# First batch normalised by halves, its conv on VectorE, and the normalised x added to the output projection by TensorE

## The chip, the cores and the metric

The kernel runs on one core of one Trainium2 chip. The metric is the device time of one execution in microseconds, median over several runs. The core's engines work side by side and hand over through semaphores: TensorE (PE in the profile; PEld is its weight load) multiplies and transposes into PSUM, VectorE (DVE) and ScalarE (ACT) work element by element, GpSimd (POOL) does small arithmetic, constants and the accumulating DMAs, SyncE (SP) issues all other DMAs.

## The reference

Two blocks with residuals over x of shape [4, 1024, 128]: a "ripple" attention and a mixture of experts, each between two layernorms. Cut to what matters here:

```python
def _ripple(x, Wqkv, Wo, conv_w):                 # C = 128, 8 heads of 16
    q, k, v = jnp.split(x @ Wqkv, 3, axis=-1)     # qh, kh, vh: the same by heads
    # each position attends to itself and to those 1, 2, 4, ..., 512 before it
    tele = einsum(softmax(q . k[pos - off]), v[pos - off])
    conv = depthwise_conv(v, conv_w)              # 7 taps, causal
    fq, fk = elu(qh) + 1, elu(kh) + 1
    low = fq @ (fk^T v) / (fq . sum(fk) + 1e-6)   # linear attention
    return (tele + conv + low) @ Wo

def _L0_attn_ref(x, ...):
    return x + _ripple(x, Wqkv, Wo, conv_w)

h = _layernorm(x)                                 # "the normalised x"
x = x + _layernorm(_L0_attn_ref(h, ...))
x = x + _layernorm(_L0_ffn_ref(_layernorm(x), ...))
```

So the normalised x enters twice: into the projections, and as the residual that is added to the output projection before the second layernorm.

## The kernel before

Everything is fp32 (the gates are spread in bf16 parts). A batch has 1,024 tokens, eight tiles (NT) of 128; a unit u is half a batch, four tiles (TPH): units 2b and 2b+1 belong to batch b. The loop over b runs five times; its pass b does the attention of batch b beside the experts (ffn) of units 2b-2 and 2b-1. Every engine has one program, written out by hand in the order in which it shall run, and waits where its operands come from another engine. Nothing is reordered: what stands behind a waiting instruction waits too.

Attention of a batch, with the names that matter:

- `stats` (VectorE, bn and mv), `ln1` (GpSimd: rstd by pow, nmr), `normalise1` (ScalarE): the normalised x, tile by tile, in `xn`. TensorE turns it (`turn_x`) into the two banks of `psA`, ScalarE copies it to `xnT`, channels on partitions. `project_k`, `project_q`, `project_v` multiply by wqkv, in the two halves of psA; ScalarE copies the results to kT, qT and vT. While batch b is at work, this head part of batch b+1 is done in between. For batch 0 it stands ahead of all.
- `features`: exp and relu of k and q on ScalarE, minimum and sum on VectorE (fkT, fqT). `token_major_v` and `token_major_fk`: turned back by TensorE and copied by ScalarE into v_tok and fk_tok. `linear_state` (TensorE, in psY) and kv (VectorE).
- `shift_v` (SyncE): 18 DMAs copy v_tok, shifted by 1 to 64 rows, into `v_shift`, 3.5 MB or so. VectorE needs them for the first `weigh`.
- `products` (VectorE, q times shifted k, three groups), `sum_heads` (TensorE), `scores` (ScalarE), `turn_scores` (TensorE), `softmax_logits` (VectorE, begins with zden), `exponentials` (ScalarE), `softmax_weights` (VectorE, begins with den), `weigh_low` and eight `weigh` (VectorE), eight `sum_terms` (TensorE, up to twelve transposes into psH, accumulated).
- The conv: `scale_taps` (ScalarE) scales vT by each of the seven taps into seven buffers (`tap_home`: convT, tapT[0], tapT[1], xnT, kexp, qexp, tapT[0] again). GpSimd adds them with six DMAs of 512 KB that accumulate in SBUF (`sum_taps_first`, `_second`, `_third`). They all run while v_shift is being filled. `features(b+1)` waits until kexp has been added.
- `add_conv(b, half)` (VectorE): hT = psH + convT. `output(b, half)` (TensorE): hT times Wo, into psY for both halves, so the second waits until the first was read. `add_normed(b, half)` (VectorE): yc = psY + xn_res, where xn_res is a copy of xn that ScalarE makes (`keep_normed`, 128x1024). `norm2(u)` (ScalarE): sums of the squares of yc. `ln2` (GpSimd), `residual(u)` (VectorE): x2 = yc * rstd2 + x_res. The residual of unit 2b stands behind the last weigh of batch b, that of unit 2b+1 in the next pass behind `products(b+1, 1)`.

After x2 come norm3, the gates, the hidden layer in psF, `experts_out` and norm4. The last units use psH and psY for gates and hidden layers too. `keep_busy` issues idle transposes of ident, into psH before the third sum of heads.

## Time and profile before

| | us |
|---|---|
| three runs | 316.63, 318.48, 319.97 |
| median | 318.48 |
| profiled execution | 320.01 |
| its span | 318.0 |

| engine | busy us | share of the span |
|---|---|---|
| PE | 256.4 | 81% |
| PEld | 173.4 | 55% |
| DVE | 234.7 | 74% |
| ACT | 205.7 | 65% |
| POOL | 90.1 | 28% |

The page's strip of 40 slices (7.95 us each), a digit is tenths busy:

```profile
PE   6664977089579779997897799989798899888894
DVE  5049936298996669889988699399976897936842
ACT  1578655047737974699869963798488615375851
PEclk9785797789959989999999969999799589799998
DMA  7300999900789940121989830106889601000003
```

DMA stands for the sixteen DMA engines together. Batch 0 is in the slices up to about the tenth; the DMA engines are full in slices 5 to 8 and VectorE's digit falls to 2 in the eighth. PEclk is the granted clock of TensorE: 10 tenths (shown as 9) are 2.4 GHz, 5 tenths 1.2 GHz.

Durations in a timeline are those of single instructions or of merged rows; neighbouring ones on an engine overlap by a tenth of a microsecond or so, so the distance from start to start is a little less than the duration. A matmul of fp32 that isn't a transpose has two records, a transpose one.

### The profile page before, as it was taken

How to read it: one execution, taken by the hardware profiler on the slowest of the kernel's cores; microseconds unless marked ns; L12 is line 12 of the kernel's file. 1: busy time of each engine (PE TensorE's matmuls, PEld its weight loads, DVE VectorE, ACT ScalarE, POOL GpSimd, SP SyncE). 2: the span in 40 equal slices, each digit the busy share in tenths (PEclk: the TensorE clock that was granted, in tenths of full speed). 3: DMA queues.
4: the chain of work that ended last, by engine and by line, in shares of the span. 5: the costliest groups of instructions: out<-in, count | busy, mean ns of one | idle time of the engine just before them, and what ended most of it. 6: DMA issues, size and time to landing. Idle time of an engine off the chain costs nothing.

```text
span 318.0 us, 4568 instructions
## 1 busy us (share of the span) xinstructions
PE 256.4 (81%) x1527; PEld 173.4 (55%) x1527; DVE 234.7 (74%) x567; ACT 205.7 (65%) x471; POOL 90.1 (28%) x153
## 2 busy tenths in 40 slices
PE   6664977089579779997897799989798899888894
PEld 6323443087345437766553448658445296774283
DVE  5049936298996669889988699399976897936842
ACT  1578655047737974699869963798488615375851
POOL 3912150101514310304566002125741103131013
PEclk9785797789959989999999969999799589799998
DMA  7300999900789940121989830106889601000003
GB/s 215 94 0 16 220 225 227 226 7 0 159 235 240 200 82 3 33 67 25 224 240 205 195 68 0 34 2 136 241 231 227 117 2 33 0 3 0 1 2 99
DMA packets 23809, 34.46 MB, mean 108 GB/s; under 512 B 3989, under 2 KB 17134, under 8 KB 23786
## 3 DMA queue, kind: packets, MB, share of 16 engines
q1 hardware_dynamic: 20330, 21.59, 24.2%
q0 software_dynamic: 3456, 12.58, 21.5%
q8 instruction: 12, 0.20, 0.3%
q14 instruction: 11, 0.09, 0.1%
HBM read 5.07 MB, written 2.10 MB: 23 GB/s over the span
## 4 chain that ended last, share of the span: by engine, by line
PE 43%; ACT 29%; SPq 8%; DVE 7%; POOL 6%; issue 3%; DMA 3%; POOLq 0%; DVEq 0%; ACTq 0%
PE psH L1215 9%; PE psA L1135 6%; PE psY L1312 5%; PE psF L1276 5%; ACT xn L633 4%; SPq L341 3%; POOL rstd L427 3%; SPq L344 3%; ACT xn L539 3%; ACT squares L626 2%; PE psY L1164 2%; PE psA L1127 2%; PE psY L1226 2%; PE psF L1255 2%; DMA v_shift<-v_tok 2%
## 5 line engine op out<-in xcount | busy, mean ns | idle before, releaser
L264 DVE TENSOR_TENSOR prods<-qT,kT 128x1024 f32<-128x1024 f32 (+1 forms) x44 | 48.8, 1166 | 13.6 <-ACT qT L527 13.6
L425 POOL TENSOR_SCALAR var<-ss 128x4 f32<-128x4 f32 (+1 forms) x25 | 11.1, 443 | 123.1 <-ACT squares L679 62.1
L1215 PE MATMUL psH<-ident,prods 128*128 128x128 f32 x324 | 43.1, 285 | 0.0
L1215 PEld LDWEIGHTS psH<-ident,prods 128*128 128x128 f32 x324 | 39.3, 149 | 2.3 <-issue 2.3
L427 POOL TENSOR_TENSOR rstd<-var,neg_half 128x4 f32<-128x4 f32 (+2 forms) x29 | 37.2, 1283 | 2.4
L902 DVE TENSOR_TENSOR prods<-v_shift,prob 128x896 f32<-128x896 f32 x32 | 35.8, 1119 | 0.0
L1276 PE MATMUL psF<-x3T,w 128*128 128x512 f32 x58 | 31.7, 661 | 0.1
L1016 DVE TENSOR_TENSOR hid<-hid,psG 128x512 f32<-128x512 f32 x32 | 20.8, 684 | 14.9 <-PE psG L1298 14.3
L1135 PE MATMUL psA<-xnT,wqkv 128*128 128x512 f32 x48 | 30.0, 771 | 2.1 <-ACT xnT L527 2.1
L1183 PE MATMUL psA<-prods,slot_sel 128*32 128x512 f32 x168 | 25.3, 656 | 4.4 <-DVE prods L264 3.0
L439 POOL DMA_DIRECT2D convT<-tapT x12 | 10.9, 907 | 60.8 <-DMA convT<-tapT 29.4
L902 DVE TENSOR_TENSOR prods<-v_tok,prob 128x128 f32<-128x128 f32 (+2 forms) x60 | 20.8, 373 | 7.5 <-DMA v_shift<-v_tok 7.5
L655 ACT ACTIVATE hid<-psF,b1c 128x512 f32<-128x512 f32 x29 | 18.8, 686 | 2.6 <-PE psF L1276 2.4
L1312 PEld LDWEIGHTS psY<-w,hid 128*128 128x128 f32 x140 | 17.7, 207 | 3.6 <-DVE prods L886 2.7
L1212 PE MATMUL psH<-ident,prods 128*128 128x128 f32 x32 | 9.7, 302 | 12.1 <-DVE prods L902 9.6
L539 ACT ACTIVATE xn<-x_in,nmr,rstd 128x128 f32<-128x128 f32 x32 | 13.0, 484 | 9.2 <-POOL nmr L436 9.2
L1312 PE MATMUL psY<-w,hid 128*128 128x128 f32 x140 | 18.0, 292 | 1.1 <-DVE prods L886 1.1
L1276 PEld LDWEIGHTS psF<-x3T,w 128*128 128x128 f32 x58 | 10.9, 210 | 14.2 <-issue 11.6
L1135 PEld LDWEIGHTS psA<-xnT,wqkv 128*128 128x128 f32 x48 | 10.6, 243 | 14.6 <-issue 6.5
L620 ACT ACTIVATE squares<-yc 128x128 f32<-128x128 f32 x32 | 9.4, 298 | 8.9 <-DVE yc L925 8.9
L1212 PEld LDWEIGHTS psH<-ident,prods 128*128 128x128 f32 x32 | 4.7, 147 | 17.6 <-DVE prods L902 13.1
L581 ACT ACTIVATE tapT<-vT,cw 128x1024 f32<-128x1024 f32 x12 | 13.2, 1135 | 0.1
(199 smaller groups left out, 557.1 us busy)
## 6 DMA issues: line engine op xcount, KB each, us to landing
v_shift<-v_tok SPq DMA_DIRECT2D x20, 448.0 KB
convT<-tapT POOLq DMA_DIRECT2D x12, 512.0 KB, 4.6
x_in<-L_attn_x SPq DMA_DIRECT2D x4, 512.0 KB, 3.6
x_res<-L_attn_x SPq DMA_DIRECT2D x4, 512.0 KB, 9.2
tapT<-xnT POOLq DMA_DIRECT2D x4, 512.0 KB, 9.9
convT<-kexp POOLq DMA_DIRECT2D x4, 512.0 KB, 7.5
tapT<-qexp POOLq DMA_DIRECT2D x4, 512.0 KB, 9.7
out<-y_out SPq DMA_DIRECT2D x7, 256.0 KB, 2.3
```

What stands on the lines that cost most here:

```text
L264: return eng.tensor_tensor(prods[:, QUADS * (s % 2) + q, t0:T], qT[:, t0:T], kT[:, PRE - off + t0:PRE - off + T], ALU.mult)
L427: return nc.gpsimd.tensor_tensor(rstd[:, cols], var[:, cols], neg_half[:, cols], ALU.pow)
L539: nc.scalar.activation(xn[:, j, :], x_in[:, j, :], ACT.Identity, bias=nmr1[:, j:j + 1], scale=rstd1[:, j:j + 1]).then_inc(xn_ready, 1)
L655: nc.scalar.activation(hid[:, c, half_cols(u)], hidden_bank(u, c), ACT.Gelu, bias=b1c[:, c:c + 1]).then_inc(hidden_free, 1)
L902: return nc.vector.tensor_tensor(dst, src.rearrange("p m (h d) -> p m h d", d=HD), w, ALU.mult)
L1016: nc.vector.tensor_tensor(hid[:, c, cols], hid[:, c, cols], psG[:, c % 2, :], ALU.mult).then_inc(gated, 1)
L1135: pe.matmul(psA[:, half, :], wqkv[:, bass.ts(part, P)], xnT[:, bass.ts(half, HALF)], start=True, stop=True).then_inc(psA_full, 1)
L1183: ins = pe.matmul(psA[32 * q:32 * q + 32, half, :], ksum_sel[:] if low else slot_sel[:, s, :], fqT[:, cols] if low else prods[:, QUADS * ( ...
L1212: pe.matmul(dst, low_terms[:, j, :], ident[:], is_transpose=True, start=True, stop=False)
L1215: ins = pe.matmul(dst, terms[:, j % TERM_BUFS, m, :], ident[:], is_transpose=True, start=False, stop=(m == live[-1]))
L1276: pe.matmul(hidden_bank(u, c), w1[:, bass.ts(c, P)], x3T[:, half_cols(u)], start=True, stop=True).then_inc(hidden_full, 1)
L1312: ins = pe.matmul(output_tile(u, n), hid[:, c, bass.ts(j, P)], w2[:, c, :], start=(c == CH - 1), stop=(c == CH - 2))
```

## The change

Three things are changed together.

1. **Batch 0's layernorm by halves.** `first_norm` (VectorE) takes statistics and variance of four tiles, then of the other four; GpSimd only does the pow (`first_rstds`), VectorE makes nmr. ScalarE normalises the first four tiles when their nmr is there. VectorE instead of ScalarE copies xnT out of PSUM.
2. **Batch 0's conv on VectorE.** `first_conv` is one multiplication by a scalar per partition and six fused multiply-adds into convT[0], each waiting for the one before: four ahead of `softmax_logits(0)`, three between it and `softmax_weights(0)`. Batch 0 has no scaled taps and no accumulating DMAs. The other batches keep theirs, with a buffer tapT[2] in place of xnT.
3. **The normalised x is added by TensorE.** xnT exists twice (by the batch's parity) and lives until the output projection. `output` issues for each tile the matmul by Wo and then a transpose of the tile of xnT that accumulates onto it. The second half goes to psH in place of psY. yc, xn_res, `add_normed` and `keep_normed` are gone; norm2 and residual read psY and psH. `keep_busy` before the third sum of heads writes to psG. Unit 6's front (turned x, gate logits, logits) uses psF, and its first hidden chunk waits until the logits have been read.

The diff's core:

```diff
             def sum_taps_first(b):
-                pool.wait_ge(tap_scaled, upto(b, TAPS, 4))
+                pool.wait_ge(tap_scaled, upto(b - 1, TAPS, 4))
...
-            ln1(0)
+            first_rstds()
             constants()
             more_constants()
-            sum_taps_first(0)
...
-            def keep_normed(b):
-
-                act.wait_ge(yc_ready, upto(b, 2, 0))
-                copy(xn_res[:], xn[:]).then_inc(xn_kept, 1)
...
             def norm2(u):
-                act.wait_ge(yc_ready, u + 1)
-                for j in unit_tiles(u):
-                    last = nc.scalar.activation(squares[:, j, :], yc[:, j, :], ACT.Square, accum_out=ss2[:, j:j + 1])
+                act.wait_ge(y_ready, u + 1)
+                for n, j in enumerate(unit_tiles(u)):
+                    last = nc.scalar.activation(squares[:, j, :], attended(u % 2)[:, bass.ts(n, P)], ACT.Square,
+                                                accum_out=ss2[:, j:j + 1])
...
+            def first_norm():
+
+                dve.wait_ge(x_in_ld, N_DMA)
+                first_chain.start(dve, 0)
+                for half in range(2):
+                    tiles = range(half * TPH, (half + 1) * TPH)
+                    cols = slice(half * TPH, (half + 1) * TPH)
+                    for j in tiles:
+                        last = nc.vector.bn_stats(bn[:, j, :], x_in[:, j, :])
+                    first_chain(last)
+                    for j in tiles:
+                        last = nc.vector.bn_aggr(mv[:, j, :], bn[:, j, :])
+                    first_chain(last)
+                    nc.vector.tensor_scalar(var1[:, cols], mv[:, cols, 1], EPS, None, ALU.add).then_inc(first_var, 1)
+                for half in range(2):
+                    cols = slice(half * TPH, (half + 1) * TPH)
+                    dve.wait_ge(first_rstd, half + 1)
+                    nc.vector.scalar_tensor_tensor(out=nmr1[:, cols], in0=mv[:, cols, 0], scalar=-1.0,
+                                                   in1=rstd1[:, cols], op0=ALU.mult,
+                                                   op1=ALU.mult).then_inc(first_normed, 1)
+                nc.vector.tensor_scalar(neg_mean[:, 0, :], mv[:, :, 0], -1.0, None, ALU.mult)
+                for half in range(2):
+                    dve.wait_ge(psA_full, filled(-1, PSA_X, half))
+                    nc.vector.tensor_copy(xnT[0][:, bass.ts(half, HALF)], psA[:, half, :]).then_inc(psA_free, 1)
...
+            def first_conv(shifts):
+
+                if 0 in shifts:
+                    dve.wait_ge(psA_free, freed(-1, PSA_V, 1))
+                    dve.wait_ge(conv_ld, N_DMA)
+                    conv_chain.start(dve, 0)
+                for shift in shifts:
+                    v, w = vT[:, VPRE - shift:VPRE - shift + T], cw[:, TAPS - 1 - shift:TAPS - shift]
+                    if shift == 0:
+                        conv_chain(nc.vector.tensor_scalar(convT[0][:], v, w, None, ALU.mult))
+                    else:
+                        conv_chain(nc.vector.scalar_tensor_tensor(out=convT[0][:], in0=v, scalar=w, in1=convT[0][:],
+                                                                  op0=ALU.mult, op1=ALU.add))
...
-            def add_normed(b, half):
...
+                    if b == 0:
+                        first_conv(range(0, 4))
                     softmax_logits(b)
+                    if b == 0:
+                        first_conv(range(4, TAPS))
...
             def linear_state(b, first):
                 if not first:
-                    pe.wait_ge(yc_ready, upto(b, 2, 0))
+                    pe.wait_ge(x2_ready, upto(b, NT, -TPH))
...
             def output(b, half):
                 pe.wait_ge(hT_ready, upto(b, 2, half + 1))
-                if half:
-                    pe.wait_ge(yc_ready, upto(b, 2, 1))
-                elif b:
+                if b and not half:
                     pe.wait_ge(out_scaled, b)
                 for j in range(TPH * half, TPH * (half + 1)):
-                    ins = pe.matmul(psY[:, bass.ts(j % TPH, P)], hT[:, bass.ts(j, P)], wo[:], start=True, stop=True)
+                    dst = attended(half)[:, bass.ts(j % TPH, P)]
+                    pe.matmul(dst, hT[:, bass.ts(j, P)], wo[:], start=True, stop=False)
+                    ins = pe.matmul(dst, xnT[b % 2][:, bass.ts(j, P)], ident[:], is_transpose=True, start=False, stop=True)
                 ins.then_inc(y_ready, 1)
...
+                    elif k >= 0:
+                        pe.wait_ge(front_free, upto(u, N_FRONT, N_FRONT - k))
```

How the instructions stand on the engines, at three places. VectorE in batch 0, before, from the last group of products (L264; ksum_sel and kv belong to the linear state) to the softmax's weights:

```order
L264 TENSOR_TENSOR prods<-qT,kT 128x1024 x6
L847 TENSOR_SCALAR ksum_sel<-head_sel,ksum 128x8
L850 TENSOR_TENSOR kv<-psY,head_mask 128x128
L858 TENSOR_SCALAR zden<-psA 128x64
L860 TENSOR_TENSOR prob<-psA,mask 128x384 x2
L867 TENSOR_REDUCE top<-prob 128x64
L868 TENSOR_TENSOR prob<-prob,top 128x768
L873 TENSOR_REDUCE den<-prob 128x64
L874 RECIPROCAL rden<-den 128x64
```

And after the change (the lines of the file are other ones):

```order
L269 TENSOR_TENSOR prods<-qT,kT 128x1024 x6
L885 TENSOR_SCALAR ksum_sel<-head_sel,ksum 128x8
L888 TENSOR_TENSOR kv<-psY,head_mask 128x128
L962 TENSOR_SCALAR convT<-vT,cw 128x1024
L964 SCALAR_TENSOR_TENSOR convT<-vT,cw,convT 128x1024 x3
L896 TENSOR_SCALAR zden<-psA 128x64
L898 TENSOR_TENSOR prob<-psA,mask 128x384 x2
L905 TENSOR_REDUCE top<-prob 128x64
L906 TENSOR_TENSOR prob<-prob,top 128x768
L964 SCALAR_TENSOR_TENSOR convT<-vT,cw,convT 128x1024 x3
L911 TENSOR_REDUCE den<-prob 128x64
```

Four conv instructions stand between kv and zden, three between the last step of the logits (prob<-prob,top) and den.

ScalarE in batch 0, before, from the copy of vT to the copy of the scores (prods is where scoresT lies):

```order
L527 ACTIVATE vT<-psA 128x512 x2
L581 ACTIVATE convT<-vT,cw 128x1024
L581 ACTIVATE tapT<-vT,cw 128x1024 x2
L581 ACTIVATE xnT<-vT,cw 128x1024
L527 ACTIVATE v_tok<-psA 128x512 x2
L527 ACTIVATE fk_tok<-psA 128x512 x2
L527 ACTIVATE xn_res<-xn 128x1024
L581 ACTIVATE kexp<-vT,cw 128x1024
L581 ACTIVATE qexp<-vT,cw 128x1024
L581 ACTIVATE tapT<-vT,cw 128x1024
L527 ACTIVATE prods<-psA 128x512 x2
```

And after:

```order
L541 ACTIVATE vT<-psA 128x512 x2
L541 ACTIVATE v_tok<-psA 128x512 x2
L541 ACTIVATE fk_tok<-psA 128x512 x2
L541 ACTIVATE prods<-psA 128x512 x2
L555 ACTIVATE xn<-x_in,nmr,rstd 128x128 x8
```

The seven scalings and the copy to xn_res are gone; v_tok follows vT at once.

TensorE at the end of batch 0, before, from the first half of the output projection (psY<-wo,prods; prods is where hT lies) to the turns of the next batch's v:

```order
L1226 MATMUL psY<-wo,prods 128x128 x4
L1135 MATMUL psA<-xnT,wqkv 128x512 x2
L1212 MATMUL psH<-ident,prods 128x128
L1215 MATMUL psH<-ident,prods 128x128 x11
L1212 MATMUL psH<-ident,prods 128x128
L1215 MATMUL psH<-ident,prods 128x128 x11
L1212 MATMUL psH<-ident,prods 128x128
L1215 MATMUL psH<-ident,prods 128x128 x11
L1226 MATMUL psY<-wo,prods 128x128 x4
L1127 MATMUL psA<-ident,vT 128x128 x8
```

And after:

```order
L1273 MATMUL psY<-wo,prods 128x128
L1274 MATMUL psY<-ident,xnT 128x128
L1183 MATMUL psA<-xnT,wqkv 128x512 x2
L1260 MATMUL psH<-ident,prods 128x128
L1263 MATMUL psH<-ident,prods 128x128 x11
L1260 MATMUL psH<-ident,prods 128x128
L1263 MATMUL psH<-ident,prods 128x128 x11
L1260 MATMUL psH<-ident,prods 128x128
L1263 MATMUL psH<-ident,prods 128x128 x11
L1273 MATMUL psH<-wo,prods 128x128
L1274 MATMUL psH<-ident,xnT 128x128
L1273 MATMUL psH<-wo,prods 128x128
```

Shown of after are the last pairs of the first half and the first of the second half; a half is four pairs of a matmul by wo and a transpose of xnT, and the second half goes to psH. The projection of the next batch's v and three sums of terms stand between the halves, as before.

## Rows read from the trace of the kernel before

**Rows 1.** The chain that ended last: start us, us, what

```profile
56.03 5.58 DMA v_shift<-v_tok
...
93.28 3.41 PE psY L1164 x16
...
97.36 0.94 ACT xn_res L527
...
160.30 1.78 PE psY L1164 x16
...
162.66 0.94 ACT xn_res L527
...
280.22 0.70 DVE yc L925
```

**Rows 2.** Timeline of VectorE in batch 0: start, us, instruction, idle before, releaser

```profile
25.97 1.23 DVE L832 SCALAR_TENSOR_TENSOR fqT<-qexp,fqT 128x1024 f32<-128x1024 f32 x1
...
39.18 0.28 DVE L850 TENSOR_TENSOR kv<-psY,head_mask 128x128 f32<-128x128 f32 x1
...
44.54 0.23 DVE L858 TENSOR_SCALAR zden<-psA 128x64 f32<-128x64 f32 x1 [5.07 <-PE psA L1127]
...
49.15 1.53 DVE L873 TENSOR_REDUCE den<-prob 128x64 f32<-128x768 f32 x1 [0.91 <-ACT prob L608]
...
61.64 0.29 DVE L902 TENSOR_TENSOR prods<-v_tok,prob 128x128 f32<-128x128 f32 x1 [7.47 <-DMA v_shift<-v_tok]
```

**Rows 3.** DMA queues, 30 to 62 us: packets, MB, share of 16 engines

```profile
q0 software_dynamic: 791, 2.91, 49.4%
...
q1 hardware_dynamic: 1994, 4.03, 46.7%
```

**Rows 4.** Timeline of SyncE's queue, first and last of 18 issues in batch 0

```profile
30.33 0.58 SPq L341 DMA_DIRECT2D v_shift<-v_tok  x1
...
56.03 0.60 SPq L344 DMA_DIRECT2D v_shift<-v_tok  x1
```

**Rows 5.** Timeline of the head, all engines

```profile
4.38 1.64 DVE L801 BATCH_NORM_STATS2 bn<-x_in 128x6 f32<-128x128 f32 x8 [0.82 <-DMA x_in<-L_attn_x]
...
6.05 0.64 DVE L805 BATCH_NORM_AGGREGATE mv<-bn 128x2 f32<-128x6 f32 x8
...
7.33 1.66 POOL L427 TENSOR_TENSOR rstd<-var,neg_half 128x8 f32<-128x8 f32 x1
...
9.31 3.19 ACT L539 ACTIVATE xn<-x_in,nmr,rstd 128x128 f32<-128x128 f32 x8 [7.24 <-POOL nmr L436]
...
11.10 0.66 PE L1127 MATMUL psA<-ident,xn 128*128 128x128 f32 x4 [2.30 <-ACT xn L539]
...
13.46 7.87 PE L1135 MATMUL psA<-xnT,wqkv 128*128 128x512 f32 x12
...
19.55 0.60 ACT L527 ACTIVATE qT<-psA 128x512 f32<-128x512 f32 x1 [0.26 <-PE psA L1135]
```

**Rows 6.** Table by stretches: busy us (instructions) per engine, PEclk, DMA share, GB/s

```profile
9.00:11.00 2.00, 0.00 (x0) 0.00 (x0) 0.00 (x0) 1.69 (x5) 1.79 (x9) 1.00 0.20 17
...
13.00:18.20 5.20, 5.20 (x10) 2.37 (x9) 0.00 (x0) 1.79 (x3) 4.33 (x24) 0.50 0.34 101
...
66.00:68.00 2.00, 2.00 (x20) 2.00 (x19) 2.00 (x5) 2.00 (x3) 0.00 (x0) 0.96 0.01 4
```

**Rows 7.** Timeline of TensorE: end of batch 0, and two projections in batch 1

```profile
71.43 1.06 PE L1226 MATMUL psY<-wo,prods 128*128 128x128 f32 x8
...
76.78 1.36 PE L1215 MATMUL psH<-ident,prods 128*128 128x128 f32 x11
...
128.14 1.88 PE L1135 MATMUL psA<-xnT,wqkv 128*128 128x512 f32 x4
```

**Rows 8.** Groups by line and form: busy us, mean ns of one, idle before

```profile
L581 ACT ACTIVATE tapT<-vT,cw 128x1024 f32<-128x1024 f32 x12 | 13.2, 1135 | 0.1
...
L1026 DVE SCALAR_TENSOR_TENSOR y_out<-psG,rstd,x 128x128 f32<-128x128 f32 x8 | 2.2, 341 | 1.2 <-POOL rstd L427 1.2
```

119 lines of the change are left out of this document (63 added, 56 removed).

## The prediction

> **What bounds the kernel now.** I read these views in this order: the chain that ended last, the timeline of each engine over batch 0, the DMA queues over the same stretch, and the table by stretches. The chain [rows 1] changes engine all the time: no engine is the bound of the whole program, so an edit is worth what it takes off this chain and nothing else. Four places of it concern the change: a DMA wait in batch 0 that ends at 61.61 us, the copy of xn into xn_res on ScalarE in batches 1 and 2 (only these two of the four copies are listed), and the addition yc on VectorE in the last batch.
>
> VectorE in batch 0 [rows 2]: from the first products to kv at 39.46 us it is busy; then it waits 5.07 us for the turned scores, 0.91 us for the exponentials and 7.47 us for the shifted copies of v. The reason for the last wait is in [rows 3]: between 30 and 62 us the software queue (the six accumulating transfers of the conv) holds 49.4% of the sixteen engines and the hardware queue (v_shift, and one x_in) 46.7%. SyncE issues the 18 transfers of v_shift from 30.33 to 56.63 us [rows 4].
>
> In the head, VectorE, GpSimd and ScalarE work one after the other before TensorE gets its first tile at 11.10 us; the projections start at 13.46 us and their last copy on ScalarE ends at 20.15 us [rows 5]. TensorE's granted clock is 1.00 in 9 to 11 us and 0.50 (1.2 GHz) from 13 to 18.2 us [rows 6].
>
> **The change part by part.** Durations are those of the profiled execution (320.0 us; span 318.0).
>
> *Head by halves.* Before: bn 1.64, mv 0.64, GpSimd's pow on eight columns 1.66, around them small ones, and xn starts at 9.31 [rows 5]. After, the first half needs 0.82 + 0.32 + about 0.2 on VectorE (var) and about 1.2 on GpSimd for four columns (between half of 1.66 and 1.66; I take 1.2), then nmr, 0.2 and hand-overs of 0.2: xn can start at 4.4 + 1.1 + 0.2 + 1.2 + 0.4 = 7.3 to 7.5. The second pow starts at about 7.2 and is there before ScalarE ends its fourth tile, so all eight tiles are 1.9 earlier. VectorE takes xnT out of PSUM in place of ScalarE, on an idle engine: nothing. Second half and projections follow: 13.46 becomes 11.35. **-2.1 us.** SyncE's queue: load_next(0) moves with xn, nothing waits for it.
>
> *TensorE's clock in the projections.* After the warm-up TensorE now waits until 11.10 us and the clock then falls. With the change it waits from 8.8 to about 9.1, works 0.7, waits 0.9 and goes on. I take it that the clock stays at 2.4 GHz. Two projections of 512 columns take 1.88 us at full clock [rows 7], four 3.6, plus the last copy 0.6: 4.2 in place of 20.15 - 13.46 = 6.7. **-2.5 us**; nothing if the clock falls all the same.
>
> The Trainium skill says in "TensorE: Matmul & The Clock Gate", Part 4, that transposes do not count as TensorE being busy for the gate, and by that the warm-up and the earlier turns could not hold the clock. This trace does not agree: in 66 to 68 us TensorE did nothing but transposes and the clock rose to a mean of 0.96 [rows 6].
>
> *ScalarE in batch 0* loses seven scalings of 1.14 us [rows 8] and one copy. Four of them, 4.2 us as they overlap, stood ahead of v_tok; TensorE's turn of v needs some 0.7 of that, so v_tok, fk_tok and SyncE's first v_shift are another 3.5 earlier. VectorE does not wait for those: it is busy up to 39.46 in any case, only moved by the head.
>
> *VectorE's conv and the transfers.* Seven instructions on 1,024 elements. Their nearest row is the fused one with two tensors, 1.23 us [rows 2]; each waits for the one before, so 1.25 from start to start, the first (one tensor) between 0.6 and 1.15. First group: 1.15 + 3 x 1.25 = 4.9, in the wait of 5.07: hidden. If TensorE should deliver the scores sooner, VectorE comes first there, no loss. Second group: 3 x 1.25 = 3.75, of which the wait of 0.91 hides one part: +2.85. What it buys: the six accumulating transfers go. v_shift starts 3.5 + 4.6 earlier, at 22, and even at the old pace (26.3 to issue, 5 to land) is there at 53 us; at its own share (0.467 x 32 = 15 us) at 39. It is needed at 61.64 - 7.47 + 2.85 - 4.6 = 52.4. So the wait of 7.47 goes, at worst but 1 us. Together 2.85 - 7.47 = **-4.6 us**. GpSimd's queue loses six issues; its ln1(1) comes earlier, which nobody waits for.
>
> *The output projection.* 32 transposes more. In the sum of a tile eleven follow each other in 1.36 us with the tail of the last, so 0.11 each [rows 7]: four are +0.44 per half. The upper bound is a matmul's own 0.27 (eight records, four matmuls, in 1.06 [rows 7]); I take the lower, since the kind is the same. Where do they lie on the path? End of batch 0: TensorE goes without a gap from the first output (71.43) over the projection of v and three sums to 78.14, and VectorE's conv addition waits for that: +0.44. The add of yc that is removed there does not help, TensorE is last. The second output of batches 0, 1 and 2 stands ahead of the turn of v, which leads to the next batch's ScalarE chain: +0.44 three times. The first output of batches 1 and 2 delays the gate spread by 0.44, and VectorE loses yc (0.7) behind it: nothing. Last batch: second output +0.44. Sum **+2.2 us**. Squares and residual now read PSUM. The nearest row is the fused instruction at the end of the kernel, with the same operands but one in PSUM: 341 ns for 128 columns [rows 8]. Should a read from PSUM cost a tenth more, that is 0.1 us for four: nothing. The bank psY is free again when residual has run, some 15 us before linear_state wants it; psH likewise.
>
> *The copies xn_res.* Two pieces of 0.94 lie on the chain [rows 1], in stretches where ScalarE goes almost without a gap up to the exponentials: **-1.9 us**. In batch 3 TensorE is last: nothing. *The last yc*: 0.73 from its start to the squares of ScalarE [rows 1]: **-0.7 us**. In the tail, hidden(6, 0) now waits for gexp, 0.4 later, and ends just before the turn of the last half: nothing, 0.3 if late.
>
> Sum: -2.1 - 2.5 - 4.6 + 2.2 - 1.9 - 0.7 = **-9.6 us**: 310.4 from the profiled execution, 308.9 from the median of 318.5. The profiled one is the slowest of four, so a part of what it shows to be gained may be its own bad luck; I forecast between the two, 309.5.
>
> **The rivals.**
> 1. *The clock falls in the projections all the same.* For it: TensorE works only 0.7 of about 1.8 us there. Against: the wait of 2.3 is gone. Time 309.5 + 2.5 = 312.
> 2. *The clock falls elsewhere.* The linear state of batch 1 took 3.41 us at half clock, that of batch 2 1.78 at full clock [rows 1], with the same instructions: 1.6 for the lower clock, and I estimate as much again for its neighbours (gate logits, turns), 3.3 in all. A chain moved by some us can put one more such stretch into batches 2 or 3: 309.5 + 3.3 to + 5.8 = 313 to 315. The other way, batch 1 loses its slow stretch: 309.5 - 3.3 = 306.
> 3. *The change doesn't do what it says*: v_shift stays as late behind VectorE as it was, because SyncE's issue and not the accumulating queue paces it. Then the wait ends at 61.64 - 4.6 - 3.5 = 53.5, since the scaling no longer holds up v_tok, and the loss is 1.1 us: 310.6. To lose the whole term the landing would have to move not at all: 309.5 + 8 = 317.5.
> 4. *Slower.* A transpose behind an fp32 matmul into the same bank may not pipeline. Five halves are on the path with four pairs each; the gain is eaten when one pair costs (9.0 + 2.2) / 20 = 0.56 us more than the matmul alone. At the matmul's own 0.27 [rows 7] it would be 309.5 + 20 x 0.16 = 312.7, and slower by over 1% needs 0.72. Nothing in the rows comes near; 323 as its time.
>
> **How the numbers follow.** Forecast 0.50 at 309.5; clock falling in the head 0.22 at 312; one more slow stretch 0.13 at 313 to 315; batch 1 at full clock 0.07 at 306; change without its main effect 0.05 at 317.5; slower 0.03 at 323. The range from 305 to 315 leaves out the last two and some edges. A measurement can tell about 1% from no change, here 315.3 and 321.7. Faster: the first four, less some edge, 0.87; same 0.09; slower 0.04, the fourth rival with a little for what I have not seen.
>
> **What would show it.** VectorE: no wait for v_shift at its first weighing, that one at about 52 us; the conv's instructions near 1.2 us, four of them ahead of zden with no or a small wait. Head: first xn near 7.4, projections from 11.4, their clock 1.00; last q copy near 15.5. TensorE: eight matmul records and four transposes of an output half within 1.6 us. No wait of ScalarE's squares for yc. Wrong would be: fused instructions well over 1.3 us; a clock of 0.5 in the projections; linear_state or low waiting for x2; a half of the output over 2 us.

## The result and the profile after

The changed kernel takes 304.35 us (median of four, 302.13 to 305.5) where the kernel before, run beside it, took 318.24 (316.63 to 319.97): 0.9554 of its time, 95% interval 0.948 to 0.963, a gain of 13.9 us. The forecast was 309.5 with a range down to 305: right in sign, wrong in size. The profiled execution took 304.41 us. Medians below are of all executions of a kernel; ratios, and the gains given with them, leave out those that were over 1.5% slower than its fastest, and are taken to the kernel before run beside it.

The page of the changed kernel: span, busy time, granted clock in tenths over 40 slices, shares of the chain.

```profile
span 302.7 us, 4600 instructions
...
PE 248.6 (82%) x1559; PEld 170.7 (56%) x1559; DVE 240.0 (79%) x573; ACT 192.6 (64%) x458; POOL 84.4 (28%) x145
...
PEclk9989599599979979999999989999999799999999
...
PE 42%; ACT 26%; DVE 21%; POOL 5%; issue 4%; DMA 1%; POOLq 0%; DVEq 0%; ACTq 0%
```

The head in its timeline, all engines; it answers to [rows 5]:

```profile
7.40 3.19 ACT L555 ACTIVATE xn<-x_in,nmr,rstd 128x128 f32<-128x128 f32 x8 [5.33 <-DVE nmr L826]
...
9.19 0.63 PE L1175 MATMUL psA<-ident,xn 128*128 128x128 f32 x4 [1.32 <-ACT xn L555]
...
11.13 5.70 PE L1183 MATMUL psA<-xnT,wqkv 128*128 128x512 f32 x12
...
15.05 0.60 ACT L541 ACTIVATE qT<-psA 128x512 f32<-128x512 f32 x1 [0.36 <-PE psA L1183]
```

xn starts at 7.40 (forecast 7.3 to 7.5), the projections at 11.13 (11.35), the last copy of q ends at 15.65 (15.5). The first products start at 15.79 in place of 20.28, 4.5 us earlier; 4.6 were forecast.

VectorE in batch 0; it answers to [rows 2]:

```profile
35.36 0.74 DVE L962 TENSOR_SCALAR convT<-vT,cw 128x1024 f32<-128x1024 f32 x1
36.13 3.93 DVE L964 SCALAR_TENSOR_TENSOR convT<-vT,cw,convT 128x1024 f32<-128x1024 f32 x3
40.96 0.23 DVE L896 TENSOR_SCALAR zden<-psA 128x64 f32<-128x64 f32 x1 [0.90 <-PE psA L1175]
...
44.60 3.92 DVE L964 SCALAR_TENSOR_TENSOR convT<-vT,cw,convT 128x1024 f32<-128x1024 f32 x3
48.55 1.53 DVE L911 TENSOR_REDUCE den<-prob 128x64 f32<-128x768 f32 x1
...
53.49 0.28 DVE L940 TENSOR_TENSOR prods<-v_tok,prob 128x128 f32<-128x128 f32 x1
```

The wait of 7.47 us for v_shift is gone, the first weighing stands at 53.49 (before 61.64, forecast 52), and the conv's fused instructions take 1.32 us from start to start (forecast 1.25). That the wait goes was forecast rightly; the first weighing came 1.5 us later than forecast.

Where the rest came from is seen when the span is cut at events that both timelines have: VectorE's two additions of the conv (add_conv) in each batch, ScalarE's gexp, VectorE's den. The last column is the prediction's sum, put into the same cuts.

| stretch | before | after | difference | forecast |
|---|---|---|---|---|
| start to second add_conv of batch 0 | 78.18 | 71.84 | -6.34 | -8.8 |
| three boundaries: second add_conv to gexp | 53.20 | 48.45 | **-4.75** | **+1.3** |
| gexp to den, batches 1 to 3 | 56.52 | 54.79 | -1.73 | -1.9 |
| den to first add_conv, batches 1 to 3 | 56.39 | 55.33 | -1.06 | 0 |
| first to second add_conv, batches 1 to 3 | 33.99 | 32.69 | **-1.30** | **0** |
| last add_conv to the end | 39.72 | 39.60 | -0.12 | -0.3 |
| span | 318.0 | 302.7 | -15.3 | -9.6 |

The error sits at the boundaries between batches and, smaller, between the two additions; in batch 0 the changed kernel gained 2.5 us less than forecast. TensorE's part of the transposes has the forecast size. The second half of the output projection of batch 0 in its timeline, before, and after (the first pair and the last, then the turn of v):

```profile
78.93 1.16 PE L1226 MATMUL psY<-wo,prods 128*128 128x128 f32 x8 [0.79 <-DVE prods L919]
79.93 1.04 PE L1127 MATMUL psA<-ident,vT 128*128 128x128 f32 x8
```

```profile
72.58 0.49 PE L1273 MATMUL psH<-wo,prods 128*128 128x128 f32 x2 [0.78 <-DVE prods L972]
72.91 0.27 PE L1274 MATMUL psH<-ident,xnT 128*128 128x128 f32 x1
...
73.91 0.27 PE L1274 MATMUL psH<-ident,xnT 128*128 128x128 f32 x1
74.02 1.04 PE L1175 MATMUL psA<-ident,vT 128*128 128x128 f32 x8
```

From the first matmul to the turn of v it is 1.44 us, and 1.00 in the kernel before: +0.44. So something else took some 6 us off the stretches in bold, less 1.48 that the third boundary of this one execution had too much (below).

### The profile page after: what moved, and what is told of

Read it like the earlier page. It is cut to its first block, busy times and chain, and to the rows that moved or that the text cites. A ratio compares the mean times of both kernels' runs of the same rounds, so it can differ in the third digit from the quotient of the medians.

```text
span 302.7 us, 4600 instructions
## 1 busy us (share of the span) xinstructions
PE 248.6 (82%) x1559; PEld 170.7 (56%) x1559; DVE 240.0 (79%) x573; ACT 192.6 (64%) x458; POOL 84.4 (28%) x145
## 4 chain that ended last, share of the span: by engine, by line
PE 42%; ACT 26%; DVE 21%; POOL 5%; issue 4%; DMA 1%; POOLq 0%; DVEq 0%; ACTq 0%
PE psH L1263 7%; PE psA L1183 5%; PE psF L1322 5%; PE psY L1358 4%; DVE prods L940 4%; ACT xn L645 3%; PE psA L1231 3%; ACT xn L555 3%; DVE prods L269 3%; PE psA L1358 3%; ACT squares L638 3%; POOL rstd L435 2%; PE psY L1212 2%; PE psA L1175 2%; POOL var L433 2%
## 5 line engine op out<-in xcount | busy, mean ns | idle before, releaser
L1263 PEld LDWEIGHTS psH<-ident,prods 128*128 128x128 f32 x324 | 39.1, 148 | 2.3 <-issue 2.3
L435 POOL TENSOR_TENSOR rstd<-var,neg_half 128x4 f32<-128x4 f32 (+2 forms) x28 | 32.3, 1155 | 2.3
L1183 PE MATMUL psA<-xnT,wqkv 128*128 128x512 f32 x48 | 26.2, 683 | 3.3 <-ACT xnT L541 3.3
L454 POOL DMA_DIRECT2D convT<-tapT x9 | 8.2, 913 | 43.3 <-DMA convT<-tapT 26.0
L1358 PEld LDWEIGHTS psY<-w,hid 128*128 128x128 f32 x140 | 16.1, 192 | 3.6 <-DVE prods L924 2.6
L1358 PE MATMUL psY<-w,hid 128*128 128x128 f32 x140 | 16.4, 276 | 1.2 <-DVE prods L924 1.2
L1183 PEld LDWEIGHTS psA<-xnT,wqkv 128*128 128x128 f32 x48 | 8.5, 203 | 13.7 <-ACT xnT L541 4.8
L1231 PEld LDWEIGHTS psA<-prods,slot_sel 128*32 128x32 f32 x168 | 5.2, 112 | 16.4 <-issue 8.5
L1367 PEld LDWEIGHTS psG<-ident 128*128 128x128 f32 x76 | 10.8, 168 | 6.3 <-issue 3.2
L1367 PE MATMUL psG<-ident 128*128 128x128 f32 x76 | 11.5, 317 | 3.1 <-POOL ident L389 3.1
```

Of the source, the lines that this page charges most:

```text
L435: return nc.gpsimd.tensor_tensor(rstd[:, cols], var[:, cols], neg_half[:, cols], ALU.pow)
L1183: pe.matmul(psA[:, half, :], wqkv[:, bass.ts(part, P)], xnT[(b + 1) % 2][:, bass.ts(half, HALF)], start=True, stop=True).then_inc(psA_full, 1)
L1231: ins = pe.matmul(psA[32 * q:32 * q + 32, half, :], ksum_sel[:] if low else slot_sel[:, s, :], fqT[:, cols] if low else prods[:, QUADS * ( ...
L1263: ins = pe.matmul(dst, terms[:, j % TERM_BUFS, m, :], ident[:], is_transpose=True, start=False, stop=(m == live[-1]))
L1358: ins = pe.matmul(output_tile(u, n), hid[:, c, bass.ts(j, P)], w2[:, c, :], start=(c == CH - 1), stop=(c == CH - 2))
L1367: pe.transpose(bank[:, bass.ts(k % TPH, P)], ident[:], ident[:])
```

## Experiments

### Each part alone

Each is one of the three pieces of the diff put into the kernel before, here in short:

```diff
+first_norm(), first_rstds()                 # head_only: in place of stats(0), ln1(0)
+first_conv(range(0, 4)), first_conv(range(4, TAPS))   # conv_only: in place of scale_taps(0), sum_taps(0)
+pe.matmul(dst, xnT[b % 2][...], ident[:], is_transpose=True, start=False, stop=True)   # add_only: no keep_normed, no add_normed
```

> Part 1 alone on the kernel before: batch 0's layernorm by halves, everything else as before. By the prediction's own steps: first products on VectorE at about 15.7 us in place of 20.28 and 4.6 us less in all (2.1 for the halves, 2.5 for the clock in the projections), since the wait for v_shift moves with it. Rival (the clock falls in the projections all the same): only 2.1 less, and a granted clock of 0.50 at 13 us.

314.64 us, ratio 0.987 (0.981 to 0.992): -4.3 us.

> Part 2 alone: batch 0's conv on VectorE, its six accumulating transfers and seven scalings gone. By the prediction: 4.6 us less (the wait of 7.47 gone, 2.85 added). By the trace of the changed kernel, where the first weighing came 3.7 us earlier from this part and TensorE then summed the first tiles at half clock: 2.5 to 3.7 less. Rival (v_shift was paced by SyncE's issue): a wait of VectorE for v_shift remains and 0 to 1 us less.

312.46 us, ratio 0.983 (0.978 to 0.988): -5.4 us.

> Part 3 alone: TensorE adds the normalised x, no yc and no xn_res. By the prediction 0.4 us less (2.2 added, 1.9 and 0.7 taken). By the trace of the changed kernel, theory G: without yc VectorE reaches its statistics earlier, so GpSimd's pow of norm3 takes 1.0 in place of 1.9 us at three batch boundaries: 0.4 + 2.3 = 2.7 us less. Theory C: what was gained at the boundaries came from TensorE's clock, which this part does not touch: 0.4 less, pow still 1.9.

313.66 us, ratio 0.985 (0.980 to 0.990): -4.8 us.

The three sum up to -14.5, all together gave -13.9: they add within their intervals. Against the forecast (-4.6; -4.6; +2.2 - 1.9 - 0.7 = -0.4) the first two are right within their intervals, and the third alone is off by 4.4 us (-4.8, interval -6.5 to -3.0). That is the term to explain.

Where it lies is read best from the traces of head_only and add_only, which from the second addition of batch 0 on differ by part 3 alone:

| stretch | head_only | add_only | difference |
|---|---|---|---|
| first to second add_conv of batch 0 | 8.93 | 9.36 | +0.43 |
| into batch 1: second add_conv to gexp | 18.06 | 16.79 | -1.27 |
| into batch 2 | 16.05 | 15.62 | -0.43 |
| into batch 3 | 16.68 | 15.88 | -0.80 |
| gexp to den, batches 1 to 3 | 56.30 | 55.53 | -0.77 |
| first to second add_conv, batches 1 and 2 | 22.24 | 21.90 | -0.34 |
| first to second add_conv, batch 3 | 11.73 | 10.83 | -0.90 |

With 0.00 from den to the first add_conv and -0.16 in the tail this makes -4.2 us, near the -4.8 of the ratio.

### GpSimd beside VectorE: a theory that is half right

In the boundary chain stands GpSimd's pow of 128 x 4 elements (norm3), behind var and ahead of nmr. GpSimd and VectorE around it, first boundary, kernel before:

```profile
85.27 1.22 DVE L832 SCALAR_TENSOR_TENSOR fqT<-qexp,fqT 128x1024 f32<-128x1024 f32 x1
...
84.73 0.68 POOL L425 TENSOR_SCALAR var<-ss 128x4 f32<-128x4 f32 x1 [2.85 <-ACT squares L626]
85.50 1.90 POOL L427 TENSOR_TENSOR rstd<-var,neg_half 128x4 f32<-128x4 f32 x1
```

The same place in the changed kernel:

```profile
78.13 1.22 DVE L868 SCALAR_TENSOR_TENSOR fqT<-qexp,fqT 128x1024 f32<-128x1024 f32 x1
...
78.82 0.58 POOL L433 TENSOR_SCALAR var<-ss 128x4 f32<-128x4 f32 x1 [3.68 <-ACT squares L638]
79.49 1.04 POOL L435 TENSOR_TENSOR rstd<-var,neg_half 128x4 f32<-128x4 f32 x1
```

The same instruction takes 1.90 and 1.04 us. The fused instruction of VectorE ends at 86.49 and 79.35: before, the pow ends 0.91 us behind it; after, var ends 0.05 behind it and the pow starts with VectorE on a one-input instruction. The Trainium skill says in "GPSIMD Engine Reference", section 1, "Specifications", that the engine shares its access to SBUF with VectorE and collides with VectorE's instructions that read two inputs there; the rows agree, and show GpSimd nearly at a stop while the fused instruction runs: of a pow that takes 1.04 us alone, 0.91 was left 1.0 us after its start. Theory G made this the cause of the gain; rival H said that VectorE's own shorter program (without yc, 0.69 us) was it. Two kernels give VectorE the same additional instruction, which moves what stands behind it by 0.50 us, once ahead of fqT and once behind:

```diff
 key_features(b + 1)
+nc.vector.reciprocal(ones_rec[:], ones[:])   # delay_early; in delay_late: behind query_features(b), b >= 1
```

> The changed kernel with one more VectorE instruction at each of the three boundaries of batches: a reciprocal of 128 x 80 elements with one input (about 0.7 us, nothing uses its result) behind the key features of the next batch, so that VectorE's fused instruction for fqT comes as late as it did before the change, when yc stood there. Theory G (GpSimd's pow of norm3 is slow beside a VectorE instruction with two inputs in SBUF): the pow of 128 x 4 takes 1.9 us again at two or three of the boundaries in place of 1.04, 1.03 and 1.36, and the kernel loses 0.9 us at each, 1.7 to 2.6 us in all, so 306 to 307 where the changed kernel takes 304.4. Rival H (the chain only got shorter because VectorE had less to do): the pow stays at 1.0 to 1.4 us, and the loss, if any, shows at VectorE's own instructions, up to 3 x 0.7 = 2.1 us.

306.86 us, ratio 0.965 (0.958 to 0.973).

> The same additional VectorE instruction (about 0.7 us, one input), now behind fqT instead of ahead of it. VectorE has as much to do as in the run with the instruction ahead. Theory G: the pow stays at 1.04, 1.03 and 1.36 us, and the kernel takes 0.9 us less at each boundary than with the instruction ahead; against the changed kernel 0 to 2 us more, by what VectorE itself is late. Rival H: as slow as with the instruction ahead, within 0.5 us.

304.58 us, ratio 0.959 (0.952 to 0.966).

With the instruction ahead the pow did not get slower, var did. GpSimd and VectorE, first boundary, delay_early:

```profile
78.95 1.22 DVE L870 SCALAR_TENSOR_TENSOR fqT<-qexp,fqT 128x1024 f32<-128x1024 f32 x1
...
79.14 1.08 POOL L434 TENSOR_SCALAR var<-ss 128x4 f32<-128x4 f32 x1 [3.69 <-ACT squares L639]
80.31 1.04 POOL L436 TENSOR_TENSOR rstd<-var,neg_half 128x4 f32<-128x4 f32 x1
```

Again var ends 0.05 us behind VectorE's instruction (80.17), so it isn't the pow as such that is slow, but whatever GpSimd instruction VectorE's one meets. What it costs depends on the boundary (second add_conv to den, us):

| | changed | delay_early | delay_late |
|---|---|---|---|
| into batch 1 | 35.35 | 35.87 | 35.36 |
| into batch 2 | 35.22 | 35.71 | 35.72 |
| into batch 3 | 32.67 | 34.23 | 33.16 |

Into batch 1 the place decides (G), into batch 2 it does not (H): wherever the instruction stands, its 0.50 us come back whole. Into batch 3 the two are 0.5 slower up to gexp, both; the rest of delay_early's is a lower clock (0.90 in 221 to 239 us). The next run takes GpSimd's collision away in the old kernel and leaves VectorE's work as it is:

```diff
-query_features(b)
-if more: stats(b + 1)
+if b and more: stats(b + 1)
+query_features(b)            # b == 0 as before
```

> The kernel before with one swap on VectorE in batches 1 and 2: the statistics of the next batch (bn_stats, bn_aggr, one input each) stand ahead of the fused fqT instruction (two inputs in SBUF) instead of behind it. Nothing is removed. Theory G' (GpSimd makes no progress while VectorE's fused instruction runs; a pow that meets it takes 1.9 us, one that does not 1.03): the pow of norm3 takes 1.0 to 1.1 us at the boundaries into batches 1 and 2 and 1.9 at the one into batch 3, which is not changed; ScalarE's xn3 follows 0.9 us earlier after its squares in the first two; -1.8 us in all (about 0.6%) against the kernel before, unless TensorE's clock blurs it. Rival P (the pow is slow in the kernel before for another reason, as the transfers or yc on VectorE): it stays at 1.9 in all three, and the time does not change.

318.19 us, ratio 1.0008 (0.9972 to 1.0044): nothing. The pow took 1.04 and 1.03 us as theory G' said, and the time did not follow (-1.8 us were expected, the interval ends at -0.9), so as the price of the gain the theory falls. The second boundary shows why. There the chain goes on over GpSimd's pow for the next batch (128 x 8). VectorE's last product ahead of it and that pow, kernel before, this run, and the changed kernel:

```profile
167.02 1.16 DVE L264 TENSOR_TENSOR prods<-qT,kT 128x1024 f32<-128x1024 f32 x1
...
168.32 1.67 POOL L427 TENSOR_TENSOR rstd<-var,neg_half 128x8 f32<-128x8 f32 x1
```

```profile
166.56 1.16 DVE L264 TENSOR_TENSOR prods<-qT,kT 128x1024 f32<-128x1024 f32 x1
...
167.86 1.67 POOL L427 TENSOR_TENSOR rstd<-var,neg_half 128x8 f32<-128x8 f32 x1
```

```profile
156.85 1.16 DVE L269 TENSOR_TENSOR prods<-qT,kT 128x1024 f32<-128x1024 f32 x1
...
158.15 1.67 POOL L435 TENSOR_TENSOR rstd<-var,neg_half 128x8 f32<-128x8 f32 x1
```

In all three the pow starts 0.14 us behind the end of the product: GpSimd stands in VectorE's two-input block, and the chain that is put down to GpSimd is paced by VectorE. From the second add_conv to the end of that product VectorE needs 21.78, 21.78 and 20.97 us: -0.81 for the changed kernel, and -0.81 is what the whole stretch to den lost (36.03, 36.03, 35.22). 0.80 of it is yc and the short wait ahead of it, as VectorE's timeline behind the key features shows, before (second addition at 146.40) and after (at 137.04):

```profile
148.34 0.69 DVE L925 TENSOR_TENSOR yc<-psY,xn_res 128x512 f32<-128x512 f32 x1
148.94 2.35 DVE L264 TENSOR_TENSOR prods<-qT,kT 128x1024 f32<-128x1024 f32 x2
```

```profile
138.78 1.22 DVE L269 TENSOR_TENSOR prods<-qT,kT 128x1024 f32<-128x1024 f32 x1
```

The first product starts 2.54 us behind the addition before, and 1.74 after. The 0.87 that the swap saved at the first pow was waited for here.

Last, the same swap in the changed kernel:

> The changed kernel with the same swap on VectorE in batches 1 and 2 (statistics ahead of the fused fqT instruction). The pow is at 1.03 us there already, but GpSimd's instruction before it (var) still takes 0.58 us beside the end of fqT. Theory G': var takes 0.2 us at the boundaries into batches 1 and 2, 0.4 us less each, -0.8 us in all, which the time can't tell and the trace can; batch 3 is unchanged. Rival: what fqT's later end delays (the scaling of tap 5, the numerators) costs as much or more: 0 to +2 us.

304.22 us, ratio 0.955 (0.950 to 0.959): no difference that can be measured. var took 0.19 us as expected, but the second unit's var, which now meets fqT, 1.23.

### The price of the transposes and of the copies

```diff
 pe.matmul(dst, hT[:, bass.ts(j, P)], wo[:], start=True, stop=False)
+pe.matmul(dst, xnT[b % 2][:, bass.ts(j, P)], ident[:], is_transpose=True, start=False, stop=False)
 ins = pe.matmul(dst, xnT[b % 2][:, bass.ts(j, P)], ident[:], is_transpose=True, start=False, stop=True)
```

> The changed kernel with each transpose of the output projection issued twice: 32 more transposes of 128 x 128 into the same banks. The normalised x is so added twice, the output differs from the reference's, and nothing else of the work changes. This prices the term of +2.2 us of the prediction (0.11 us each, 0.44 us per half, five halves on the path) by itself. If it is right: 0.44 us more per half at the records, +2.2 us in all, 306.6. If the transposes lie in slack of the chain or keep TensorE's clock up: 0 to +1 us. If a pair costs more than the matmul's records say: over +3 us.

307.81 us, ratio 0.968 (0.961 to 0.975): +3.5 us by the medians, +3.3 by the spans. Each transpose is 0.11 us from start to start again; the parts are +0.43 between the conv additions of batch 0, +0.29, +0.45 and +1.13 at the boundaries (into batch 3 the pow meets fqT again, 1.90 us instead of 1.36), +0.29, +0.29 and +0.48 between the conv additions of batches 1 to 3. So the price of one transpose was right and the places were not. Of the five halves that the forecast had on the path, two cost their 0.44 (batch 0, and 0.44 in the last batch), the one into batch 1 0.29, the one into batch 3 1.13, and the one into batch 2 nothing: what it costs up to gexp is back at den (35.22 us from the second addition, with the transposes once or twice), since VectorE is last there. The three halves that the forecast had at nothing cost 0.29, 0.29 and 0.48. All together the run gave over 3 us where the term had 2.2. (The medians compared here are of executions made at different times; by the ratios, 0.968 and 0.955, whose intervals just touch, the distance is 4 us.)

```diff
 if b:
+    copy(xn[:], xn[:])
     scale_taps(b, range(5, TAPS))
```

> The changed kernel with ScalarE's copy of 128 x 1,024 elements put back in batches 1 to 3 where xn was copied to xn_res (it copies xn onto itself; the result is the same). It prices the term of -1.9 us. If it is right: gexp of batch 1 to its denominators 19.3 us instead of 18.4, batch 2 0.4 to 0.95 us longer, batch 3 nothing; 1.4 to 1.9 us in all, 306. Rival: in the changed kernel ScalarE has slack there, and the copy costs nothing.

306.1 us, ratio 0.964 (0.960 to 0.968). From gexp to den it takes 0.96, 0.29 and 0.19 us more in batches 1 to 3: 1.4 of the 1.9 that were forecast.

### The conv and the transfers

```diff
-first_conv(range(0, 4)), first_conv(range(4, TAPS))     # VectorE
+token_major_fk(b); scale_taps(0, range(0, 4))           # ScalarE; six accumulating DMAs as before
```

> The changed kernel, but with batch 0's conv as in the kernel before (taps scaled by ScalarE, summed by six accumulating transfers), only that ScalarE scales taps 0 to 3 behind the copies of v_tok and fk_tok instead of ahead of them; VectorE does no conv. It asks how much of the gain at the wait for v_shift needs the conv on VectorE at all. Theory D (v_shift was late because it was issued late and shared the sixteen engines): v_shift starts at about 22 us instead of 30, takes about 31 us as before beside the accumulating transfers and lands at about 53; VectorE is there at 50 and waits 3 to 4 us; first weighing at 53 to 54, as in the changed kernel (53.7): same time within 1 us. Rival (the accumulating transfers alone made it late): the first weighing stays at 57 us or more, 3 us slower. Rival (only the order mattered): v_shift lands before 50, no wait, 3.5 us faster.

303.84 us, ratio 0.958 (0.952 to 0.963), as fast as the changed kernel, but not as theory D had it. VectorE's timeline at den and at the first weighing:

```profile
47.67 1.54 DVE L928 TENSOR_REDUCE den<-prob 128x64 f32<-128x768 f32 x1 [4.04 <-ACT prob L630]
...
52.62 0.28 DVE L957 TENSOR_TENSOR prods<-v_tok,prob 128x128 f32<-128x128 f32 x1
```

There is no wait for v_shift at 52.62, though all six accumulating transfers run: the first shifted copy is issued 7.8 us earlier (22.58, before 30.33 [rows 4]) and the last 14.8 us earlier (41.23, before 56.03), for nine of the eighteen are issued before the first accumulating transfer, at 28.98. So the lateness of v_shift was one of order: ScalarE scaled taps ahead of v_tok. Starting earlier is not enough by itself: in head_only v_shift starts at 25.77, with the accumulating transfers beside it from the start, and VectorE waits 8.68 us.

What VectorE waits for at den is ScalarE's exponentials, and these the transfers do hold up, by another way. ScalarE has no scaling left to do (the last ends at 37.26), but stands before the next batch's xn, which needs GpSimd's nmr; and GpSimd's program waits until an accumulating transfer has landed, issues the one that builds on it, and only then comes to that nmr:

```profile
43.72 3.18 ACT L566 ACTIVATE xn<-x_in,nmr,rstd 128x128 f32<-128x128 f32 x8 [4.61 <-POOL nmr L453]
46.81 0.83 ACT L630 ACTIVATE prob<-prob 128x768 f32<-128x768 f32 x1
```

```profile
40.01 0.86 POOL L456 DMA_DIRECT2D tapT<-qexp  x1 [2.52 <-DMA tapT<-tapT]
```

The wait of 4.04 us is 3.1 more than the 0.91 of the kernel before, about what VectorE's second group of conv instructions costs in the changed kernel; that is why the two are equally fast.

```diff
-first_conv(range(4, TAPS))
+nc.scalar.activation(tapT[n][:], vT[...], ACT.Copy, scale=cw[...])             # taps 4 to 6
+nc.gpsimd.dma_start(tapT[0][:], tapT[1][:], accum_op=ALU.add)                  # and tapT[2]
+nc.gpsimd.dma_start(convT[0][:], tapT[0][:], accum_op=ALU.add)
```

> The changed kernel with VectorE doing only taps 0 to 3 of batch 0's conv (in its wait for the scores); ScalarE scales taps 4 to 6 behind fk_tok and GpSimd's queue adds them by three accumulating transfers. It prices the second group of three fused instructions, for which the prediction put +2.85 us. If that is right and the transfers of v_shift keep out of the way: the first weighing at 50.8 us in place of 53.7 and the kernel 2.8 us faster, 301.5. If three accumulating transfers make v_shift late again: a wait at the first weighing, 53 us or later, no gain. If they make the sum of the conv late: a wait at the first addition of the conv.

299.36 us, ratio 0.941 (0.938 to 0.944): faster than the changed kernel by 1.5% on the ratios, and by more than the 2.8 us expected. GpSimd does the next batch's nmr ahead of the three transfers here, and the wait for the exponentials is back at its 0.91 us:

```profile
44.50 1.53 DVE L929 TENSOR_REDUCE den<-prob 128x64 f32<-128x768 f32 x1 [0.91 <-ACT prob L632]
```

From zden to den it is 4.64 us, 7.59 in the changed kernel: the second group of three conv instructions cost 2.95 (forecast 2.85), and here it isn't needed. In the traces zden comes another 1.1 us earlier (39.86 for 40.96; 40.1 in three other traces of the changed order), and the stretch of the first sums, from the first weighing of shifted v to the second addition, takes 16.51 us for 18.15, with TensorE's clock at half for 3.4 us around them in place of 6.8: that part is not the conv's price.

### TensorE's clock

Into batch 1, the clock of the kernel before is at half from 8.5 to 18.7 us behind the second add_conv (86.7 to 96.9 us of the execution); in the changed kernel for 3.4 us (84.7 to 88.2). Tables by stretches, before and after:

```profile
83.00:94.00 11.00, 6.37 (x27) 2.89 (x28) 10.96 (x29) 6.69 (x24) 3.94 (x5) 0.67 0.92 231
86.70:96.90 10.20, 7.98 (x33) 5.15 (x26) 8.15 (x24) 2.99 (x7) 2.06 (x4) 0.50 0.84 233
```

```profile
80.00:84.00 4.00, 0.96 (x9) 0.54 (x6) 3.97 (x16) 3.04 (x6) 1.89 (x4) 1.00 0.93 250
84.00:88.00 4.00, 4.00 (x17) 3.43 (x18) 3.73 (x7) 0.60 (x1) 0.00 (x0) 0.59 0.84 245
53.00:62.00 9.00, 7.17 (x39) 7.17 (x40) 7.93 (x15) 1.57 (x2) 0.00 (x0) 0.62 0.00 0
```

(The last row is a loss of the changed kernel: the first sums of batch 0 ran at a mean clock of 0.62, and the stretch from the first weighing of shifted v to the second add_conv took 18.15 us for 16.33.) Three runs filled TensorE's waits at boundaries with idle transposes of the identity, and a fourth, further down, lengthened the warm-up:

```diff
+keep_busy(9, psG[:, 1, :])       # after_fill: all three boundaries, none in batch 0; old_fill_1, split_fill_1: b == 1 alone
 sum_heads(b, 0)
+keep_busy(9, psG[:, 1, :])
 turn_x3(u0)
```

> The changed kernel with nine filling matmuls (into a bank that is overwritten afterwards, their result is not used) ahead of the first sum of each batch's heads and ahead of the turn of x3 at the boundaries, in time that TensorE waits. Theory C (what is left of the clock's loss lies in these stretches): the granted clock, 0.949 over the span of the changed kernel, rises, and the stretch around the first sum of batch 0 (53 to 62 us, clock 0.62) goes from 9.0 us to some 7.5, the one of batch 2 (172 to 181 us, 0.81) is 1 us shorter: -2 to -3 us in all, 302. Rival: the fillings come where TensorE is needed and their own time (9 x 0.22 us at full clock) is lost: +1 to +3 us.

307.37 us (303.18 to 309.11), ratio 0.957 (0.947 to 0.968): no gain. The first boundary took 15.32 us for 16.96, the others 17.58 and 17.57 for 15.61 and 15.88. The stretch of 53 to 62 us was not tested: no filling stands in batch 0, and yet its clock was 0.81 in this trace for 0.62.

> The kernel before with nine filling matmuls (their result is not used) ahead of the first sum of batch 1's heads and nine ahead of the turn of x3 behind it, in time in which TensorE waits for VectorE and ScalarE; nothing else, and at this one boundary alone. In the kernel before TensorE's clock is at half from 8 to 15 us after the second addition of the conv of batch 0 there (18.99 us from that addition to gexp). Theory C (the half clock of this stretch was 1.5 to 2 us of the boundary's loss, and the changed kernel lost a part of it by the earlier turn of its work): with the fillings the clock stays at 1.00 and the stretch takes 18.99 - 2.5 = 16.5 us; the kernel 2 to 3 us less, 315.5 to 316.5. Rival: the fillings come where TensorE is wanted (18 x 0.11 = 2 us) and give nothing.

318.07 us, ratio 1.0019 (0.998 to 1.006). The clock stayed at full over the first sum (0.98 in 84 to 92 us) and fell right behind it (0.61 in 92 to 96), for 3.4 us in place of 10.2. The stretch took 17.50 us, where head_only and old_warm, with 10.2 us of half clock, have 18.06 and 17.96: 0.5 us, not 2.5, and no gain in the median. Theory C fails for the old kernel.

```diff
-WARM_UP = 28
+WARM_UP = 40
```

> The kernel before with 40 filling matmuls in the warm-up instead of 28, so that TensorE works until its first turn of xn at 11.1 us instead of waiting 2.3 us. This prices the term of -2.5 us (the first projections at 2.4 instead of 1.2 GHz) without the head by halves. If it is right: granted clock 1.00 from 13 to 18 us, the last copy of q ends at 17.6 us instead of 20.15, and the kernel takes 2.5 us less, 316. Rival: the wait between the turns and the projections brings the clock down all the same, 0.50 and no gain.

317.78 us, ratio 0.997 (0.993 to 1.001). The clock held and q was there at 17.55 us, as forecast:

```profile
13.00:18.00 5.00, 5.00 (x14) 1.83 (x13) 0.32 (x1) 3.47 (x7) 4.44 (x25) 1.00 0.35 105
```

Yet the median moved by 0.9 us and not 2.5. The profiled execution had the clock at half from 11.6 to 18.4 us ([rows 6] show a part); those of add_only, conv_only, old_stats_first and old_fill_1, with the same head, for 3.4 us each (13.2 to 16.6 in old_fill_1), and their first products start at 19.0 to 19.4 us, not at 20.28. So the loss there is smaller in most executions than in the one that was read. The same holds for the third boundary: 18.15 us in the profiled execution, 16.67 or 16.68 in the five kernels with the old addition (head_only, conv_only and the last three of the old kernel).

> The changed kernel with VectorE's conv of batch 0 cut to taps 0 to 3 as in the conv_split run (299.4 us), and in addition the eighteen filling matmuls at the first boundary. In the run with fillings at all boundaries the first took 15.3 instead of 17.0 us while the other two lost 1.7 to 2.0 each, for their clock was full already. So here -1.6 us against the conv_split run: 297.8. Rival: the clock is full there in most executions without the fillings, and they cost 0 to 1 us.

297.72 us, ratio 0.938 (0.935 to 0.941), six runs from 297.3 to 298.4, the fastest kernel of the study; from conv_split (0.938 to 0.944) the ratios don't part it for certain. At this boundary of the new order the fillings hold the clock all through:

```profile
69.00:82.00 13.00, 9.94 (x78) 6.70 (x80) 12.97 (x30) 8.91 (x29) 3.44 (x6) 1.00 0.93 224
```

The boundary takes 15.33 us, 16.96 without them. There TensorE does not wait for VectorE's sum operands as long as before (0.76 us behind the first fillings, 2.00 in old_fill_1).

Put side by side, the traces show how much of this boundary goes with the clock. In the new order it takes 15.33 us with no half clock in it (split_fill_1, after_fill), 16.96 with 3.4 us (changed, conv_split), 18.16 with 6.8 us (taps_after_v); in the old order 17.50 with 3.4 us (old_fill_1) and 17.96 to 18.98 with 10.2 us.

## Why the prediction was wrong

- *Head by halves and its clock, -4.6*: right within its interval, -4.3 alone (-6.1 to -2.4). The part that was the clock, -2.5, was what the profiled execution lost (6.8 us at half, 3.4 in four others); by itself it gave -0.9 (-2.2 to +0.4).
- *Conv and v_shift, -4.6*: right as a number, -5.4 alone (-6.9 to -3.9), though in part by luck. Of the -4.9 at the first weighing in conv_only's trace, 1.1 stand already at the first products (19.17 for 20.28, the head's clock), so 3.8 is the conv's own; another 0.8 came in batch 3 (below). The reason given, that the six transfers must go, was not the point: with v_tok copied first they can stay (taps_after_v), but then they hold up GpSimd's nmr.
- *The sum over batch 0, -8.8*: -6.3 in the traces of the table. TensorE's half clock over the first sums of the profiled execution is a part of it: four traces whose kernels are the same up to there (changed, after_fill, new_copies, new_stats_first) have the second addition at 69.6 to 71.8 us. What fell short here covered a part of the gain that was missed elsewhere.
- *Output projection, +2.2*: one transpose is priced rightly (0.11 us), their places on the path in part (turn_twice: over 3 us for the 2.2), which makes the miss of this part larger and not smaller. The failed step is the line beside them, that the removal of yc and of its add is worth nothing: "TensorE is last" for batch 0 (right there, +0.43), "VectorE loses yc (0.7) behind it: nothing" for the first outputs of batches 1 and 2, and for the second outputs, at the three boundaries, yc is not counted at all. I looked at what stands directly behind yc and not at VectorE's block up to the next point at which GpSimd and ScalarE wait for it. Three boundaries were forecast at +1.3 and gave -2.5 between head_only and add_only. Into batch 2 VectorE alone sets the time to den: yc and its wait take 0.80 us of its block, the stretch lost 0.81, the transposes cost nothing, and 0.50 us put back on VectorE cost 0.49 and 0.50. Into batch 3 it is 16.68 to 15.88 (another 1.48 is the profiled execution's own slow clock), and 0.50 us put back cost 0.5 again up to gexp, at either place. Into batch 1 it is from between 17.5 and 19 down to 16.96; that one changes with the clock in every kernel. No run takes away or puts back yc alone, so the 0.80 at the three boundaries rests on the timelines and on the delay runs.
- *First to second add_conv, 0*: in batches 1 and 2 also the yc step. VectorE's addition of the first half stands there between weighings, and the stretch got 0.17 shorter in spite of 0.44 of transposes. In the last batch it got 0.95 shorter, but most of that is not yc: conv_only, where yc stays, has 10.97 us there, against 11.74 before and 10.79 after. Before, VectorE waited for TensorE's sums; in conv_only it does not:

```profile
278.28 0.69 DVE L919 TENSOR_TENSOR prods<-psH,convT 128x512 f32<-128x512 f32 x1 [0.68 <-PE psH L1215]
```

```profile
270.56 0.68 DVE L996 TENSOR_TENSOR prods<-psH,convT 128x512 f32<-128x512 f32 x1
```

Part 2 alone makes this wait go, and so does part 3 alone (10.83). TensorE's clock was at half for 10.2 us ahead of it in all five traces with the old conv and the old addition, and for 3.4 us in conv_only; but after_fill has 10.2 us there too and no wait, so why it goes stays open.
- *Copies, -1.9*: 1.4 by the run that puts them back, 1.73 in the table. *The last yc*: right with its transposes, -0.12 for -0.3.
- *Rival 2 downward* (batch 1 loses its slow stretch, 306, chance 0.07) is the one that came, in part; it should have had more, since the change shortens the very wait ahead of that stretch (TensorE waits 1.75 us for VectorE's products ahead of the first sums of batch 1, 2.98 before). Its 306 is near the measured 304.35 by luck in part: it put all of the difference down to the clock.

What remains open: how much of the first boundary's gain is clock and how much VectorE and GpSimd. At 3.4 us of half clock the old order has 17.50 us (with fillings) and the new one 16.79 to 16.97, so 0.5 to 0.7 would be the order's; the rest goes with the clock, and why the new order keeps it up is not shown. The runs that were to part them in the old kernel (old_stats_first, old_fill_1) moved single stretches in their traces by 0.5 to 1.5 us and the median not at all; the 58 runs of the kernel before that were made beside the experiments lie between 314.8 and 323.1 us, at mean granted clocks from 0.889 to 0.919, and a gain of 1 us in one stretch shifts where the clock falls later.
